# Attention in fp32 row tiles, exponentials over four PSUM banks, sums from a ones column, and no scratch in DRAM

## What is computed

```
Q = (t @ rot) @ Wq.T;  K = (t @ ent) @ Wk.T;  V = t @ Wv.T
dist2 = sum(Q*Q)[:, :, None] + sum(K*K)[:, None, :] - 2 * Q @ K.T
scores = exp(-dist2)
attn = softmax(scores, axis=-1)      # a second exponential
out = attn @ V                       # 400 tokens, 32 channels, 32 batches
```

## Time and profile before

| | |
|---|---|
| runs | 222.94, 222.96, 223.4 us, median 222.96 |
| span of the profiled execution | 221.9 us (its own time is not listed; the median lies 1.06 us above the span) |
| PE busy | 198.5 us (89%), 1182 instructions |
| PE weight loads | 97.9 us (44%) |
| ACT busy | 169.1 us (76%) |
| DVE busy | 161.2 us (73%) |
| POOL busy | 29.8 us (13%) |
| DMA | 21.95 MB, mean 99 GB/s |
| mean granted clock of TensorE | 0.966 |

### The profile page before, as it was taken

How to read it: one execution, slowest core, us unless ns; L and a number is a source line. 1 busy time by engine, 2 the same in 40 slices (tenths; PEclk the granted TensorE clock), 3 DMA queues, 4 the chain that set the end, 5 groups by cost and what they waited for, 6 DMA issues and landing times. The chain is left out here.

```text
span 221.9 us, 3477 instructions
## 1 busy us (share of the span) xinstructions
PE 198.5 (89%) x1182; PEld 97.9 (44%) x1182; DVE 161.2 (73%) x294; ACT 169.1 (76%) x307; POOL 29.8 (13%) x44
## 2 busy tenths in 40 slices
PE   6858999999999869699999999999999997699950
PEld 6733655646546335123243434334343332376630
DVE  0559289989989926978685777859596865765980
ACT  4083798799599799988989989898989954445630
POOL 7000000450330160432020000101010000000000
PEclk9999999999999999979999999999999999579995
DMA  6940200357348050880627162443500000000016
GB/s 183 370 149 15 74 1 0 98 220 200 123 150 219 20 222 3 273 194 6 167 58 190 38 155 71 117 111 85 140 0 3 0 0 0 3 3 0 0 65 234
DMA packets 20229, 21.95 MB, mean 99 GB/s; under 512 B 2062, under 2 KB 17102, under 8 KB 20084
## 3 DMA queue, kind: packets, MB, share of 16 engines
q1 hardware_dynamic: 20212, 21.73, 33.5%
HBM read 14.74 MB, written 6.96 MB: 98 GB/s over the span
## 5 line engine op out<-in xcount | busy, mean ns | idle before, releaser
L508 ACT ACTIVATE arena<-ps 128x800 f32<-128x800 f32 (+1 forms) x56 | 44.6, 798 | 5.8 <-PE ps L1066 5.3
L515 ACT ACTIVATE arena<-arena 128x800 f32<-128x800 f32 (+1 forms) x56 | 46.5, 831 | 0.0
L1066 PE MATMUL ps<-qa,ka 128*128 128x400 bf16 (+1 forms) x128 | 35.4, 340 | 2.0 <-ACT arena L508 1.9
L1066 PE MATMUL ps<-qb,kb 96*128 96x400 bf16 (+1 forms) x128 | 35.4, 338 | 0.0
L742 DVE TENSOR_TENSOR psum<-arena 128x400 f32<-128x400 f32 x32 | 19.6, 612 | 14.3 <-ACT arena L515 14.3
L742 DVE TENSOR_TENSOR psum<-psum,arena 128x400 f32<-128x400 f32 x32 | 19.5, 608 | 6.0 <-ACT arena L515 4.6
L1066 PEld LDWEIGHTS ps<-qa,ka 128*128 128x128 bf16 (+1 forms) x128 | 10.4, 97 | 26.1 <-ACT arena L508 13.7
L1099 PE MATMUL ps<-arena,vb 128*32 128x400 f32 x192 | 21.6, 527 | 0.3 <-issue 0.3
L751 DVE RECIPROCAL arena<-ps 128x400 f32<-128x400 f32 x7 | 18.5, 2650 | 0.0
L661 DVE COPY arena<-arena 32x400 f32<-32x400 f32 x48 | 17.2, 358 | 0.9
L587 ACT ACTIVATE yb<-ps 128x160 f32<-128x160 f32 x36 | 10.9, 303 | 9.1 <-PE ps L1183 6.8
(11 more groups left out here) (148 smaller groups left out, 360.9 us busy)
## 6 DMA issues: line engine op xcount, KB each, us to landing
ka<-dk SPq DMA_DIRECT2D x32, 100.0 KB
qa<-dq SPq DMA_DIRECT2D x32, 100.0 KB
dk<-arena SPq DMA_DIRECT2D x8, 300.0 KB, 2.2
dq<-arena SPq DMA_DIRECT2D x8, 300.0 KB, 2.6
arena<-x_tok SPq DMA_DIRECT2D x4, 400.0 KB
t<-x SPq DMA_DIRECT2D x1, 1600.0 KB, 11.4
kb<-dk SPq DMA_DIRECT2D x16, 100.0 KB
qb<-dq SPq DMA_DIRECT2D x16, 100.0 KB
```

The source lines that it names most:

```text
L508: nc.scalar.activation(prob[par][:, lo:hi, :], ps[:, o:o + hi - lo, 0:N], ACT.Exp, scale=2.0).then_inc(e1_done, 1)
L515: nc.scalar.activation(p, p, ACT.Exp).then_inc(p_ready, 1)
L1066: last = mm_(ps[row:row + keys, bank, 0:N], kk[par][0:rows, b, o:o + keys], qq[par][0:rows, b, :], start=first, stop=not first, skip_group ...
```

## The change

The attention is rewritten and its helpers with it.

- K and Q stay in fp32 where ACT copies them (kf, qf), batch b on partitions 32b to 32b+31. `scores` makes one fp32 matmul of 32 rows for each batch, four row tiles, each into a bank of its own (0 to 3), and four bf16 matmuls of 6 rows for the squared norms (ek, eq). The last tile is four tiles of 32 x 32 into bank 4 (`tail_scores`). A unit is now four tiles, and there is one set of score banks.
- ACT's exponentials go over the four banks, 1600 elements, and 400 for the last tile.
- The values carry a column of ones in place of channel 31. PE sums the weights with them; DVE copies the product (`unscaled`, us); one matmul spreads the sum (`spread_sums`), another mixes the values with w2, which now holds Wv (`mix_values`). DVE's additions and the sums go. value_products uses the identity in place of Wv.
- The parts, the rests and the stores and loads through DRAM go. The squared norms are put in place by 16 DMAs of 3 rows a pair, from SBUF to SBUF (`spread_entropies`); on SP those of pair 0 stand ahead of load_tokens(3).
- All eight tap copies are on DVE.
- PE waits for w2 ahead of the second mix_v.

```diff
-UNITS = (TILES + 1) // 2
-ADDS = NB * (FULL - 1)
+UNITS = FULL + 1
...
+            for i in range(2):
+                sp.wait_ge(v_mixed, 2 * i + 2)
+                load_tokens(i + 1)
+            spread_entropies(0)
+            sp.wait_ge(v_mixed, 6)
+            load_tokens(3)
+            for i in range(1, PAIRS):
+                spread_entropies(i)
...
-                    act.wait_ge(zp_ready, 2 * i + par + 1)
-                    for k in ACT_TAPS:
-                        last = nc.scalar.copy(*tap_input(par, 1, k))
-                    last.then_inc(u_act, 1)
                     z_part(par, 96, P, ACT.Identity).then_inc(plain_ready, 1)
...
+            def inner(g, q):
+
+                act.wait_ge(s_done, UNITS * g + q + 1)
+                if q < FULL:
+                    src, dst = ps[:, 0:NB, 0:N], prob[g % 2][:, NB * q:NB * q + NB, :]
+                else:
+                    src, dst = ps[:, TAIL_BANK, 0:N], prob[g % 2][:, TILES - 1, :]
+                nc.scalar.activation(dst, src, ACT.Exp, scale=2.0).then_inc(e1_done, 1)
...
+                inner(g, 0)
+                if g > 2:
+                    norm2(g - 3, 1)
+                outer(g - 1, 2)
+                if g > 2:
+                    norm2(g - 3, 2)
+                inner(g, 1)
+                outer(g - 1, 3)
+                outer(g, 0)
+                inner(g, 2)
+                outer(g, 1)
+                if g > 1:
+                    norm2(g - 2, 0)
+                inner(g, 3)
...
-                            if j == 0 or k not in ACT_TAPS:
-                                last = nc.vector.tensor_copy(*tap_input(par, j, k))
+                            last = nc.vector.tensor_copy(*tap_input(par, j, k))
...
             add_x(0)
+            dve.wait_ge(w2_made, 1)
+            nc.vector.tensor_copy(w2[:, :], ps[:, 4, 0:P]).then_inc(w2_ready, 1)
...
+            def unscaled(g):
+
+                dve.wait_ge(pv_done, g + 1)
+                if g > 0:
+                    dve.wait_ge(w2_done, g)
+                nc.vector.tensor_copy(us[:, :], ps[:, PV_BANK, 0:N]).then_inc(us_ready, 1)
...
             taps(0)
+            pe.wait_ge(w2_ready, 1)
             for i in range(PAIRS - 1):
...
+            def scores(g, q):
+
+                if q == 0:
+                    pe.wait_ge(q1_ready, g + 1)
+                    pe.wait_ge(e_in, 16 * E_LOADS * (g // 2 + 1))
+                    if g > 0:
+                        pe.wait_ge(e1_done, UNITS * (g - 1) + FULL)
+                else:
+                    pe.wait_ge(e1_done, UNITS * g + q)
+                for b in range(NB):
+                    mm_(ps[:, b, 0:N], kf[C * b:C * b + C, g, P * q:P * q + P], qf[C * b:C * b + C, g, :],
+                        start=True, stop=False)
+                for b in range(NB):
+                    r = slice(C * b, C * b + 2 * EP)
+                    last = mm_(ps[:, b, 0:N], ek[r, g, P * q:P * q + P], eq[r, g, :], start=False, stop=True)
                 last.then_inc(s_done, 1)
...
+            def spread_sums(g):
+
+                pe.wait_ge(us_ready, g + 1)
+                if g > 0:
+                    pe.wait_ge(nrm_ready, g)
+                mm_(ps[:, SUM_BANK, 0:N], last_row[:, :], us[:, :], start=True, stop=True).then_inc(spread_done, 1)
+
+            def mix_values(g, bank=SUM_BANK):
+
+                if bank == SUM_BANK:
+                    pe.wait_ge(rden_ready, g + 1)
+                mm_(ps[:, bank, 0:N], w2[:, :], us[:, :], start=True, stop=True).then_inc(w2_done, 1)
...
             for g in range(1, G):
...
+                scores(g, 1)
+                products(g - 1, 1)
+                if g > 1:
+                    mix_values(g - 2)
+                if g > 2:
+                    project2(g - 3)
+                scores(g, 2)
+                tail_scores(g)
+                products(g - 1, 2)
+                tail_products(g - 1)
+                if g > 1:
+                    center2(g - 2)
+                if g < G - 1:
+                    scores(g + 1, 0)
+                spread_sums(g - 1)
+                products(g, 0)
+                if g > 1:
+                    variance2(g - 2)
```

More of the change, by code:

```diff
@@ L560, in _ @@
-            for step, first, end in ((squares, 0, 2), (inverse_roots, 2, 3), (kq_firsts, 3, 5),
-                                     (v_and_squares, 5, UNITS)):
-                step(PAIRS - 1)
-                for u in range(first, end):
-                    inner(0, 0, u)
-                    if u:
-                        outer(0, 0, u - 1)
+                inner(g, 0)
[4 more added lines that the diff above has]
+                    norm2(g - 3, 2)
@@ new lines, in weights @@
+                inner(g, 1)
[6 more added lines that the diff above has]
+                inner(g, 3)
+            squares(PAIRS - 1)
+            inner(0, 0)
+            inverse_roots(PAIRS - 1)
+            inner(0, 1)
+            outer(0, 0)
+            kq_copies(PAIRS - 1)
+            inner(0, 2)
+            outer(0, 1)
+            v_and_e(PAIRS - 1)
@@ L1118, in variance2 @@
-            def variance2(g, banks=NORM_BANKS):
+                mm_(ps[:, bank, 0:N], c_("center"), t0[:, g, :], start=True, stop=True).then_inc(centered2, 1)
+            def variance2(g, bank=NORM_BANK):
                 pe.wait_ge(sq2_ready, g + 1)
-                mm_(ps[:, banks[0], 0:N], c_("mean"), sq2, start=True, stop=True).then_inc(var2_done, 1)
-            PRODUCTS_AT = (1, 2, 4, 5)
-            def attend(g, par):
-                since = g if isinstance(g, int) else G
-                for u in range(UNITS):
-                    scores(g, par, u)
-                    if since > 0 and u in PRODUCTS_AT:
-                        products(g - 1, 1 - par, PRODUCTS_AT.index(u), first=since == 1)
-                    if since > 0 and u == 3:
-                        sums(g - 1, 1 - par, first=since == 1)
-                        tail_sums(g - 1, 1 - par)
-                    if since > 1 and u == 4:
-                        center2(g - 2)
-                    if since > 1 and u == 5:
-                        project2(g - 2)
-                    if since > 1 and u == 6:
-                        variance2(g - 2)
@@ L1143, in _ @@
-            pe.wait_ge(operands_in[0], LOADED)
-            for step, first, end in ((center, 0, 2), (variance, 2, 3), (project_kq, 3, 5), (project_v, 5, UNITS)):
-                step(PAIRS - 1)
-                for u in range(first, end):
-                    scores(0, 0, u)
-            pe.wait_ge(v_ready, G + CREDIT)
-            pe.wait_ge(es_ready, G + CREDIT)
-            for g in range(1, G):
-                pe.wait_ge(operands_in[g % 2], LOADED * (g // 2 + 1))
-                attend(g, g % 2)
@@ new lines, in project2 @@
+            def project2(g, bank=NORM_BANK):
+                if bank == NORM_BANK:
+                    pe.wait_ge(ln2_ready, g + 1)
+                mm_(ps[:, bank, 0:N], wc[:, :], t0[:, g, :], start=True, stop=True).then_inc(wx_done, 1)
+            center(PAIRS - 1)
+            scores(0, 0)
+            variance(PAIRS - 1)
+            scores(0, 1)
+            project_kq(PAIRS - 1)
+            scores(0, 2)
+            project_v(PAIRS - 1)
+            pe.wait_ge(v_ready, G)
+            tail_scores(0)
```

486 lines of the change are left out of this document (172 added, 314 removed).

## The result

The changed kernel takes **228.94 us** (median) against 223.18 of the kernel before in the same series: a ratio of **1.025, 95% interval 1.020 to 1.031**. All ratios here leave out executions more than 1.5% above the fastest of their kernel (one of 237.4 us here, the rest are 228.06 to 229.14), while medians and ranges hold all of them. The forecast was 221.5 us and slightly faster, with 228 as the upper end of its range: the direction was wrong, and the time lies outside the range. The profiled execution took 228.74 us with a span of 226.9, so what follows explains 226.9 against 221.9.

What follows compares the result with a forecast made beforehand. PE was taken to bound the kernel, with ACT 0.6 us behind a group. +2.5 + 0.7 − 2.7 − 4.1 + 2.2 = −1.4 gave a 220.5 span, with 1.06 around it 221.5 us against 222.96; range 215.5 to 228.

Steps and rivals of the forecast that it cites:

- The sixteen small DMAs on SP: Ahead of load_tokens(3): 0.35 us each, load out at 54, mix_v(3) due 6 us later; cost 0, bound 0 to 3.
- The four tap copies and the wait for w2: First pair: taps end 1.45 us later, w2's copy follows add_x, mix_v(1) starts near 24.3 instead of 21.72; together +2.5 us.
- The pairs: PE waits 0.6 to 0.7 us for DVE's copies, entropies gain 0.34: +0.4 a pair, two of three pairs, +0.7 us.
- The ramp: Last pair's centre to group 0's last product, 28.7 us before: −2.7 us; falling clock taken as 0, bound +1.
- The score blocks: Four fp32 row tiles priced like four column tiles: 0.93 us a block and for the last tile; bounds 0.83 and 3.4.
- The groups: Attention loop, groups 1 to 6: 71.1 us before, 67.0 after, with a period of 11.5 us: −4.1 us.
- The ring: Chain of dependent steps through ACT and PE in each group, score banks no longer doubled: sets the period at 11.5 us.
- The end: Group 6's last product to the aggregate: 14.8 us before, 17.0 after, with spread, copy, logarithm, exponential, quotient in a row: +2.2.
- 3 and 5: 3: last tile's four tiles queue at one bank, 239, chance 0.05. 5: no row tile runs beside another, about 300, 0.02.
- rival 1: In the loop the ring gives way and PE's own 10.8 us set the group: 217.5 us, chance 0.23.
- Rival 2: Row tiles overlap only in part, 1.2 us a score block: 226.8 us, chance 0.16.
- Rival 4: Fixed costs win: start and end paid in full, ramp at the low clock: 222.5 to 224 us, chance 0.16.

Runs made afterwards that it cites:

- the later logarithm: Changed kernel with ScalarE's logarithm of norm moved behind the outer exponential, directly ahead of its own exponential: 228.02 us median, ratio 1.013.
- the four edits: Changed kernel with pair 3's load first, two tap copies on ScalarE, w2 wait at center(0), later logarithm of norm: ratios 0.983, then 0.988.

## Why the prediction was wrong, by its own steps

**The sixteen small DMAs on SP: the largest error.** The step said "at 0.35 each the load goes out at 54", cost 0, bound 0 to 3. Each issue took 0.69 us, the load left at 60.5, and PE waited 2.36 (shown by the edit that puts the load first: 2.43 us back). The bound named just this case, and I still put 0 in the sum. The price came from one DMA between DRAM and SBUF, the new ones go from SBUF to SBUF, and I carried it over without keeping the bound in the forecast's own range. Whether it is the source or another trait of these DMAs that doubles the price was not tested.

**The four tap copies and the wait for w2.** Predicted +2.5 at the start; between mix_v(0) and mix_v(1) it is 15.92 against 13.20 us, +2.72. The mechanism and its size were right. What was missed lies ahead of it: mix_v(0) itself is 1.03 us late. The first product of the preparation, in the kernel before, the changed kernel, and the changed kernel's second profile:

```profile
5.56 0.42 PE L918 MATMUL ps<-prep 100*100 100x100 f32 x2 [0.69 <-DVE prep L627]
5.65 0.65 PE L808 MATMUL ps<-prep 100*100 100x100 f32 x2 [1.03 <-DVE prep L563]
6.06 0.42 PE L808 MATMUL ps<-prep 100*100 100x100 f32 x2 [1.44 <-DVE prep L563]
```

In the changed kernel's first profile these products take 0.65 us for what took 0.42. That looks like the lower clock, though the windows show a granted clock of 1.00 there. But the second profile has 0.42 again behind a longer wait, starts mix_v(0) at 9.19 and has the slow stretch only then. Over all profiles of kernels with the change mix_v(0) starts between 8.76 and 9.78. So it is 0.2 to 1.3 us later than before by the execution, and how much of that is the change's doing is open.

**The pairs: +0.4 each, measured +0.83.** With GpSimd's tail values out of the way it is 18.09 − 17.70 = +0.39. The step was right and lacked a neighbour: tail_values moved from the loop to the side of the tap copies, and the prediction gave it no cost there. Also the "third pair loses nothing": center(2) to center(3) takes 17.00 against 16.61, +0.39 there as well. The start, the pairs and the load held on SP together make the 8.2 us where 3.2 were predicted.

**The ramp: −2.7, measured −2.3; right.** The clock stayed at 1.00 there in this execution, as forecast. Its bound of +1 was too small: in the five profiles of edited kernels in which the clock fell there, it cost 1.6 to 4.6 us. That the forecast's 0 held here is luck.

**The score blocks: the mis-sized term of the loop.** 0.93 was predicted, 1.06 measured; the last tile 0.97 for 0.93. Row tiles with 128 weight columns take 0.78 us where I used the 0.67 of a full product; the bf16 part and the change of shape take 0.28 as assumed. The Trainium skill, "TensorE: Matmul & The Clock Gate", section "Measured speedup vs the span model", gives 1.19 by the prediction's estimate from its 3.07: the measured block lies between. Its rule of one PSUM bank for different row tiles ("TensorEngine Tiling (Array Packing)", section "Restrictions and Gotchas") does not show in the time here: four row tiles that write one bank finish in 129.27 − 128.30 = 0.97 us with their bf16 part, no more than four that write four banks (though those have 128 weight columns and not 32).

**The groups: −4.1, measured −2.0.** The ring was named link by link and was what set the period, which the later logarithm shows (11.98 to 11.39). Its terms add up to 11.46 and it was 0.52 short: 2 × 0.13 and 0.04 by the blocks, 0.11 by the last product (0.78 for 0.67) and 0.11 by the spread (0.87 for 0.76). ACT's links and the variance with the step to ACT came as forecast (3.89 for 3.9, 0.97 for 0.96). The last two errors are one: I charged a change of tile shape only behind a block. The rows have 0.67 for a full product between its likes, 0.76 to 0.78 with another shape on one side (130.08 to 130.86, 130.86 to 131.62) and 0.86 to 0.87 with another shape on both, as the spread (132.68 to 133.55) and the variance (134.36 to 135.22) have it. The same error stands in PE's own sum: 10.6 to 10.8 predicted, 11.39 without any wait. The ring was short by half a microsecond a period, in five periods, and it took away the gain inside the loop: at 11.98 the new group costs what the old one cost. The forecast treated ten links as exact to 0.05 each; the only rival for a longer ring was that of the row tiles.

**The end: +2.2, measured +2.3; right.** The recurrence behind it was 1.1 us shorter than before, which I had not seen: from the aggregate to the end it is 31.0 us at a mean granted clock of 0.85, and was 32.1 at 0.82, so by the windows some 9.3 us ran at the lower of the two levels and not 11.6. No run asks why.

Of the rivals, 3 and 5 are refuted by the rows above, and rival 1 too, since the logarithm comes late. Rival 2 has its place and direction (a block of 1.06 us) but only half its price. Rival 4 has the start and the end right, the ramp's clock not in this execution, and its 224 is too low. The way it really went, a load held behind cheap-looking DMAs, was in the list of costs and among the signs of being wrong ("a wait on x_tok"), and in no rival.

## What to carry to other kernels

When work moves to a queue, price the queue by an instruction of the same kind (its source, its destination), and ask what stands behind it; if no such row exists, the bound belongs into the range and not beside it. A ring through two engines is broken by moving one operation that nobody needs yet, and a single swapped line gave what removing a DRAM round trip had not. Removing work from DVE and the DMAs gave nothing here while PE and ACT held each other. And a wait of some 2.3 us on TensorE cost 1.2 to 4.6 us more in the profiles in which the clock fell behind it, so fill such waits if the work around them can't be moved.

## What the runs showed that I had not expected

- The same kernel at the same place ran at a granted clock of 1.00 in one execution and of 0.83 in another (5 to 25 us), and the ramp of the four edits took 26.9 us in one profile and 28.5 in another. The wait of 2.2 us alone does not decide it, but no stretch whose waits had been filled showed a low clock in its profiled execution (5 to 25 us in two profiles, the ramp in three, the wait for the tokens in one).
- An SBUF to SBUF DMA of three rows holds SP for 0.69 us, twice the 0.31 of a load from DRAM.
- Leaving four bf16 matmuls (0.28 us with the change of shape behind them) out of a block gained 0.18. A full fp32 product takes 0.67 us among its likes, 0.76 to 0.78 with another tile shape on one side and 0.86 to 0.87 with one on both.
- Eight copies of 32x400 on DVE take 2.98 us alone and 3.43 beside two small GpSimd operations of 0.45 to 0.52 us.
